# Query and key projections of two self attentions issued together in a unit's first tile

## What is computed

```python
q, k, v = x @ Wq, x @ Wk, x @ Wv        # 16 heads of 128
q, k = rope(q), rope(k)                 # layer 0 only
scores = where(causal, NEG_INF, q @ k.T * scale)
ctx = softmax(scores) @ v
x = layernorm(x + ctx @ Wo)
```

## Time and profile before

| | us |
|---|---|
| median of 3 runs | 2787.59 |
| lowest, highest | 2781.76, 2787.94 |
| profiled execution, device time | 2783.47 |
| its span from first to last instruction | 2781.6 |
| first unit's first maximum to last unit's, `self0` | 36.49 to 461.19 |
| the same, `self1` | 1458.66 to 1822.8 |

### The profile page before, as it was taken

The page is one execution under the profiler, slowest core; times in us unless marked ns, Lnnn a source line. Parts: engine busy times, 40 slices in busy tenths (PEclk is TensorE's granted clock), DMA queues, the critical chain, the costliest instruction groups (busy, mean ns, idle before and its releaser), DMA issues. The chain is left out here.

```text
span 2781.6 us, 59030 instructions
## 1 busy us (share of the span) xinstructions
PE 2475.6 (89%) x21768; PEld 1595.1 (57%) x21768; DVE 1857.3 (67%) x3317; ACT 1568.3 (56%) x2742; POOL 863.3 (31%) x741
## 2 busy tenths in 40 slices
PE   6888888989999999999789999999999999968454
PEld 4556554456666666664456666654666666634221
DVE  4767775157777777771566666625888888849776
ACT  4666664057878778781335555512777777723221
POOL 4565664501111101122232212241001100256674
PEclk9999999999999999999889999999999999988677
DMA  3333333225665655673403343330877777841000
GB/s 88 85 70 82 82 71 83 69 54 115 108 118 115 113 111 107 115 134 102 159 1 85 92 89 91 87 91 16 152 147 146 146 144 145 165 113 42 21 0 30
DMA packets 752868, 263.27 MB, mean 95 GB/s; under 512 B 724816, under 2 KB 724816, under 8 KB 751184
## 3 DMA queue, kind: packets, MB, share of 16 engines
q1 hardware_dynamic: 750960, 255.48, 43.9%
q0 software_dynamic: 1760, 5.77, 0.7%
HBM read 82.84 MB, written 2.10 MB: 31 GB/s over the span
## 5 line engine op out<-in xcount | busy, mean ns | idle before, releaser
L793 ACT ACTIVATE ph<-p,ri 128x1024 bf16<-128x1024 f32 (+4 forms) x512 | 437.3, 854 | 477.7 <-DVE ri L1065 398.0
L1075 DVE SCALAR_TENSOR_TENSOR pl<-p,ri,ph 128x1024 bf16<-128x1024 f32 (+4 forms) x512 | 513.5, 1003 | 143.0 <-issue 76.9
L1132 PE MATMUL ps<-wo_hi,v_hi 128*128 128x128 bf16 x2688 | 478.5, 220 | 61.1 <-DMA wo_lo<-pl 60.6
L1134 PE MATMUL ps<-wo_hi,v_lo 128*128 128x128 bf16 x2688 | 478.1, 220 | 0.0
L1133 PE MATMUL ps<-wo_lo,v_hi 128*128 128x128 bf16 x2688 | 478.0, 219 | 0.0
L804 ACT ACTIVATE p<-p,nb 128x1024 f32<-128x1024 f32 (+4 forms) x512 | 435.6, 851 | 46.3 <-DVE nb L1058 36.3
L1132 PEld LDWEIGHTS ps<-wo_hi,v_hi 128*128 128x128 bf16 x2688 | 263.4, 98 | 130.8 <-DMA wo_lo<-pl 81.7
L1132 PE MATMUL ps<-k_hi,q_hi 128*128 128x512 bf16 (+3 forms) x768 | 271.9, 354 | 36.6 <-DVE k_lo L1028 27.4
L1133 PEld LDWEIGHTS ps<-wo_lo,v_hi 128*128 128x128 bf16 x2688 | 263.6, 98 | 38.9
L1133 PE MATMUL ps<-k_lo,q_hi 128*128 128x512 bf16 (+3 forms) x768 | 271.7, 354 | 0.0
L1134 PE MATMUL ps<-k_hi,q_lo 128*128 128x512 bf16 (+3 forms) x768 | 271.7, 354 | 0.0
(11 more groups left out here) (197 smaller groups left out, 6011.0 us busy)
## 6 DMA issues: line engine op xcount, KB each, us to landing
raw_kv<-in_wkvself SPq DMA_DIRECT2D x32, 512.0 KB, 4.0
raw_q<-in_wqself SPq DMA_DIRECT2D x32, 256.0 KB, 2.6
wo_hi<-ph SPq DMA_TRANSPOSE x512, 3.1
wo_lo<-pl SPq DMA_TRANSPOSE x512, 3.1
raw_q<-in_woself SPq DMA_DIRECT2D x32, 256.0 KB, 2.8
raw_q<-in_wqcross SPq DMA_DIRECT2D x32, 256.0 KB, 2.8
raw_q<-in_wocross SPq DMA_DIRECT2D x32, 256.0 KB, 3.0
raw_kv<-in_wkvcross SPq DMA_DIRECT2D x24, 256.0 KB, 3.1
```

The source lines that it names most:

```text
L793: nc.scalar.activation(m["ph"][:, qt % 2, 0:w], m["p"][:, qt % 2, 0:w], ACT.Copy, scale=ri[:, qt % 2:qt % 2 + 1]).then_inc(p_norm, 1)
L1075: nc.vector.scalar_tensor_tensor(out=m["pl"][:, qt % 2, 0:w], in0=m["p"][:, qt % 2, 0:w], scalar=ri[:, qt % 2:qt % 2 + 1], in1=m["ph"][:, ...
L1132: nc.tensor.matmul(o, l(0), r(0), start=first, stop=False)
L1134: return nc.tensor.matmul(o, l(1), r(0), start=False, stop=last)
```

## The change

Query and key jobs stand in tile 0; tiles 1 and 2 have none, and the value job stays in tile 3. The order of the jobs among each other stays Q, K, V. The same line serves both self attentions and the stretch ahead of unit 0.

```diff
         else:
-            plan = [[("Q", 0)], [("K", 0)], [], [("V", 0)]]
+            plan = [[("Q", 0), ("K", 0)], [], [], [("V", 0)]]
         return plan[qt]
```

## The result

The kernel became slower: 2843.26 us in the median of 4 runs (2840.57 to 2846.2), against 2785.12 (2781.76 to 2787.94, 4 runs) for the kernel before. The ratio is 1.0209, with a 95% interval of 1.0196 to 1.0222. The profiled execution took 2840.76 us, 57.3 more than the one shown before; its span is 2838.9 us.

| stretch | before, us | after, us | change |
|---|---|---|---|
| start to unit 0's first maximum, `self0` | 36.49 | 33.91 | -2.6 |
| units 0 to 30 of `self0` | 424.70 | 467.24 | +42.5 |
| from there to `self1`'s first maximum | 997.47 | 997.83 | +0.4 |
| units 0 to 30 of `self1` | 364.14 | 378.16 | +14.0 |
| from there to the end of the span | 958.8 | 961.8 | +3.0 |

What follows compares the result with a forecast made beforehand. It took DVE and ACT, handing tiles back and forth, to bound the first self attention and PE the second. Its terms, 53 - 2 + 7 + 7 = +65 us on 2783.47, gave 2849 us, range 2815 to 2878.

Steps and rivals of the forecast that it cites:

- PE's waits are slack in the first self attention: First self attention: finished scores lay some three microseconds before DVE read them, so DVE and ACT set the pace.
- The first rival: PE sets the pace; the `k_lo` waits vanish, at most 25.6 us go, giving 2758 us; chance 7%.
- The key's sum comes no earlier, and two queues stand before it: First self attention: POOL's sum only 0.1 us earlier, ACT and DVE queued behind it; 1.3 us per unit without a split.
- The second rival: Idle time of DVE and ACT absorbs the moved wait; -2 to +12 us, 2782 to 2796; chance 6%.
- The split units: First self attention, units where POOL splits weights: tile 1's remainder meets a piece; 1.3 + 0.9 = 2.2 us each.
- The 2.4 us that the prediction worked out by that rule: Alternative cost per split unit if DVE's remainder could end only after POOL's piece; 3 us more in the sum.
- the bound of 1.1: Split units: upper limit in us on the extra delay if tile 1's remainder is held to the piece's end.
- Covered work: First self attention: the key projection on PE ends 0.4 us before ACT needs it; priced at 0, bounded by 9 us.
- The gain ahead of unit 0: Before unit 0, ACT's copy goes ahead of the query's rounding, ending POOL's idle time; -1.9 us, once.
- two terms of 7 us: Second self attention: 0.4 us in each of 17 units without weight loads, 0.5 in each of 14 with loads.
- tile 0's transposes leave later: Second self attention: tile 0's reciprocal moves later, delaying SP's queue; 0.5 us per unit with loads, between 0 and 1.1.
- the third rival: Longer PE waits in the first self attention bring the lower clock, slowing the key projection; adds 21 us, 2870; chance 12%.

Runs made afterwards that it cites:

- run 1: Changed kernel, but in the first self attention the key's rounding (ACT) and remainder (DVE) again stand behind tile 2's softmax step; 2797.08 us.
- run 8: Kernel before, with PE alone issuing the key's matmuls right behind the query's, in the first self attention only; 2789.37 us.
- Runs 1 and 4: Besides run 1: the changed kernel with POOL's product and sum of the key's rotation on 256 of the 512 columns; 2812.06 us.
- run 6: Changed kernel, but in the first self attention POOL begins a unit's weight pieces only after tile 1's remainder; 2829.43 us.
- run 5: Kernel before, with POOL's product and sum of the key's rotation on 256 of the 512 columns; 2785.0 us.
- run 2: Kernel before, with the new plan in the second self attention alone; 2804.02 us, 1.0067.
- Run 10: Kernel before, second self attention only: PE issues the key's matmuls behind the query's, DVE takes tile 0's remainder ahead of tile 1's maximum; 2792.29 us.
- run 7: Kernel before, with the new plan in the first self attention alone, the key's rounding and remainder kept at the end of tile 2; 2779.8 us, 0.9979.
- run 11: As run 7, and in the second self attention DVE takes tile 0's remainder ahead of tile 1's maximum; 2779.99 us, 0.9991.

## Why the prediction held, point by point

**PE's waits are slack in the first self attention.** Right, and shown: with PE's order of the changed kernel, run 1 gives the loss of this stage back and run 8 costs 4.6 us. The waits of PE came out at 88 us where they had been 58, while the time that decides lies in two queues. The first rival (2758 us) is excluded by the result's sign. What it got right is that the wait for `k_lo` goes. The slack has an end, as units 12 and 20 of run 8 show.

**The key's sum comes no earlier, and two queues stand before it.** Right: it comes 0.26 us earlier (0.1 expected), `k_hi` waits 2.27 us ("about 2"), and a unit without a split grows by 1.24 us in the mean of units 8 to 26 (13.29 to 14.53; 1.3 expected). Runs 1 and 4 show the mechanism from two sides: behind tile 2's step the wait is gone, and with a shorter chain on POOL each unit is shorter by as much. The second rival, that idle time takes the wait up, fell with them.

**The split units** were the term of the wrong size. They grew by 1.71 us (13.73 to 15.45), not 2.2. The step that failed: "I take the measured 1.53 - 0.62 = 0.9, so 1.3 + 0.9 = 2.2 us". The 0.9 us was set on top of a unit time that held a part of that delay already: unit 19 took 13.79 against 13.35 for unit 20, 0.44 more, and this part was not taken off. The 0.9 itself was right: after the change a unit with a split takes 15.45 - 14.53 = 0.92 us more than one without. 0.9 - 0.44 on top of 1.24 gives 1.70, close to the 1.71 measured. That the delay is tile 1's remainder meeting the second piece was right: 1.50 against 0.48 us, and run 6 removes it.

The Trainium skill (SBUF — State Buffer, Who interferes with whom) has a VectorE instruction with two SBUF inputs blocked until a GpSimd instruction that reads SBUF and began earlier has ended, and the runs agree: `k_lo` in run 5 begins 0.15 us behind the piece, ends 0.54 behind its end, and so takes 2.56 us instead of 0.69. The 2.4 us that the prediction worked out by that rule was too large by 0.7 us, for the same reason. The remainder itself lost 1.50 - 0.48 = 1.02 us, between the 0.9 that was taken and the bound of 1.1.

**Covered work.** The key projection was priced at nothing, and ACT waited for it for 2.0 us in all. PE's wait for the bank, 29.1 us in 25 places, is the cover being used. The gain ahead of unit 0 was 2.6 us, with 1.9 expected.

**The second self attention.** The size was right (14 us expected; 14.0 in the profile, 17 in run 2), but by luck: it was the sum of two terms of 7 us, and both missed. The 17 units without weight loads cost 12.2 us (0.7 each, where 0.4 was expected) and the 14 with loads 1.8 (0.1 each, where 0.5 was expected); in run 2 it was 10.8 and 5.8. Tile 3's scores wait for tile 1's maximum as described, in nearly every unit, but for 0.2 us each and not 0.4:

```profile
PE ps L1132 <- DMA wo_lo<-pl: 17.2, 19, 1.8
PE ps L1132 <- DVE nb L1056: 5.6, 29, 1.0
```

In a unit without loads another wait comes later. Unit 20 took 11.28 us before and 11.6 after; SP's transpose of tile 0's low half, ACT's rounding of tile 2's probabilities and its copy of the values there, before:

```profile
1700.17 1.18 SPq L418 DMA_TRANSPOSE wo_lo<-pl  x1
...
1702.52 0.62 ACT L793 ACTIVATE ph<-p,ri 128x384 bf16<-128x384 f32 x1 [0.36 <-DMA wo_lo<-pl]
...
1704.54 0.60 ACT L741 ACTIVATE v_hi<-ps 128x512 bf16<-128x512 f32 x1 [0.58 <-PE ps L1134]
```

and after:

```profile
1749.41 1.17 SPq L418 DMA_TRANSPOSE wo_lo<-pl  x1
...
1751.75 0.61 ACT L793 ACTIVATE ph<-p,ri 128x384 bf16<-128x384 f32 x1 [1.57 <-DMA wo_lo<-pl]
...
1752.97 0.57 ACT L741 ACTIVATE v_hi<-ps 128x512 bf16<-128x512 f32 x1
```

Before, the copy of the values waited for PE. After, PE is done by then, and the chain that ACT and DVE still have to run hangs on tile 0's transposes, for which the rounding of tile 2 waits 1.57 us. The transpose starts 6.02 us behind the unit's first maximum (1743.39), before 4.86 us behind it (1695.31), as tile 0's reciprocal now stands behind the key's remainder. So "tile 0's transposes leave later" was right, but the prediction priced it only in units with loads and through PE's waits, where it comes through ACT's. This is read from the trace; no run of this part took that wait away. Run 10 doesn't speak against it, as ACT and DVE keep the old plan there. Open is why units with n mod 4 equal to 3, in which POOL splits weights, grew by 1.0 us and those with 0 by 0.3 (units 8 to 27).

**The clock.** PE was granted 0.98 of its full clock over units 0 to 30 of the first self attention in either kernel; the third rival didn't come. The windows from the first unit's to the last unit's first maximum, before and after (busy us of PE, PEld, DVE, ACT, POOL; PEclk; DMA share; GB/s):

```profile
36.49:461.19 424.70, 363.43 (x3516) 240.38 (x3514) 294.37 (x680) 278.72 (x618) 259.88 (x194) 0.98 0.35 78
```

```profile
33.91:501.15 467.24, 369.02 (x3516) 239.72 (x3513) 301.58 (x682) 280.49 (x618) 252.21 (x192) 0.98 0.32 70
```

A mechanism of its kind, a stretch at the lower clock that PE has no longer the time for, is seen in units 12 and 20 of run 8.

**Sum.** -2.6 + 42.5 + 14.0 + 3.4 = 57.3 us on the profiled execution, with 65 expected. The first self attention is 10.4 us below its 53: 8.5 in the units with a split (22.3 for 30.8) and 1.9 in the others (20.2 for 22.1). The 3.4 us outside both stages, which make up for a part of this, are of the size by which runs of one kernel differ.

## What to carry to other kernels

When work is moved earlier, look up what it hands over to: here the chain behind it (four operations on POOL, one after the other) was no sooner done, but the wait for its result had moved ahead of other work in two in-order queues, and that cost 1.2 us a unit. Move the start of a chain and leave its end where it was: the same move with the last two steps in their old place gave the loss of the first self attention back and left the kernel 0.2% below the one before (run 7; run 11, with one more step, could not confirm it). And when a delay is added to a unit's time that was read from the trace, take off what of that delay the unit already holds.

## What was not expected of the hardware

POOL and DVE delay each other both ways. In unit 20 of the changed kernel the query's sum on POOL took 1.27 us; the key's, begun at 340.79 while DVE's `q_lo` ran until 341.18, took 1.52. `q_lo`, begun at 340.10 while POOL's product ran until 340.63, took 1.08 us, where it takes 0.69 nearly alone (run 5). Half the columns save POOL somewhat less than half: 1.27 us for a product of 128 x 512 and 0.73 for one of 128 x 256 (run 5). And a piece of work on POOL that starts earlier can cost DVE more than it gains: in run 5 a shorter rotation moved the weight pieces under `k_lo`, which then took 2.56 us instead of 1.02 in the kernel before (unit 19).
